# First layer's normalised tokens: turned by VectorE in 32x32 blocks and placed by sixteen transfers, instead of by TensorE

## The reference, cut to what matters

```
x_norm = (x - mean(x)) * rsqrt(var(x) + 1e-6) * ln_scale + ln_bias      # per token, over 128 channels
qkv    = x_norm @ w_qkv + b_qkv                                          # [1024, 128] @ [128, 384]
attn   = softmax(q k^T / 4) over all 1024 tokens, 8 heads of 16
x      = x + (attn v) @ w_out + b_out
```

## Time and profile before

| | us |
|---|---|
| median of three runs | 796.75 |
| the profiled execution | 800.51 |
| its span, first to last instruction | 798.8 |
| TensorE busy (PE) | 758.7 (95%) |
| ScalarE busy (ACT) | 605.2 (76%) |
| VectorE busy (DVE) | 504.5 (63%) |
| GpSimd busy (POOL) | 160.9 (20%) |

### The profile page before, as it was taken

One profiled execution on the slowest core, in us unless ns is written; L12 is line 12 of the kernel. 1 busy time (PEld: TensorE's weight loads), 2 busy tenths in 40 slices (PEclk: granted clock), 3 DMA queues, 4 the chain that ended last, 5 costly groups with the idle time before them and its releaser, 6 DMA issues.

```text
span 798.8 us, 14130 instructions
## 1 busy us (share of the span) xinstructions
PE 758.7 (95%) x4973; PEld 360.5 (45%) x4973; DVE 504.5 (63%) x1512; ACT 605.2 (76%) x686; POOL 160.9 (20%) x198
## 2 busy tenths in 40 slices
PE   8889999999999999999999999999999999898977
PEld 4422333345443545345443545345453455233655
DVE  6514445778467675678657775677726784456864
ACT  4598879787887788787897788878887877777313
POOL 2630504320341020410330212410310201100000
PEclk9999999999999999999999999999999999999999
DMA  2544333432443241622523332422414422400100
GB/s 67 104 78 91 63 62 80 91 63 45 81 95 59 48 80 42 132 51 42 98 61 78 61 61 61 116 51 48 76 32 107 67 48 47 112 6 2 34 1 27
DMA packets 44732, 51.32 MB, mean 64 GB/s; under 512 B 15728, under 2 KB 33776, under 8 KB 44656
## 3 DMA queue, kind: packets, MB, share of 16 engines
q1 hardware_dynamic: 44656, 50.35, 32.6%
HBM read 5.45 MB, written 4.19 MB: 12 GB/s over the span
## 4 chain that ended last, share of the span: by engine, by line
PE 59%; ACT 17%; DVE 6%; issue 6%; ACTq 0%; DVEq 0%
PE O L658 20%; PE S L643 15%; ACT Pr L921 12%; PE BC L672 6%; PE BC L790 3%; PE BC L664 2%; PE BC L713 2%; PE BC L772 2%; PE BC L691 2%; PE A L596 2%; ACT hT L970 1%; ACT tT L936 1%; ACT L921 1%; ACT L970 1%; PE A L672 1%
## 5 line engine op out<-in xcount | busy, mean ns | idle before, releaser
L921 ACT ACTIVATE Pr<-S 128x1024 f32<-128x1024 f32 x512 | 493.0, 1029 | 114.0 <-PE S L643 110.2
L658 PE MATMUL O<-Pr,Va 128*32 128x512 f32 x2048 | 253.5, 602 | 1.1 <-ACT Pr L921 0.9
L643 PE MATMUL S<-Qs,Ks 49*128 49x512 f32 x1024 | 217.3, 469 | 18.0 <-ACT Pr L921 16.0
L643 PEld LDWEIGHTS S<-Qs,Ks 49*128 49x128 f32 x1024 | 87.6, 184 | 178.3 <-ACT Pr L921 138.8
L658 PEld LDWEIGHTS O<-Pr,Va 128*32 128x32 f32 x2048 | 50.3, 109 | 105.4 <-issue 97.5
L1147 DVE STREAM_TRANSPOSE OT<-O 128x512 f32<-128x512 f32 x32 | 22.8, 714 | 54.5 <-PE O L658 54.3
L1252 DVE TENSOR_REDUCE r<-BC 128x1 f32<-128x512 f32 x56 | 36.0, 684 | 21.1 <-PE BC L713 21.1
L485 POOL TENSOR_SCALAR xn<-X,ln 128x128 f32<-128x128 f32 x56 | 44.1, 800 | 4.0 <-DVE ln L1060 4.0
L516 POOL TENSOR_TENSOR squares<-qh 128x1024 bf16<-128x1024 f32 x7 | 13.3, 1895 | 154.3 <-DVE hot L1274 117.8
L524 POOL TENSOR_TENSOR q1l<-q1T,q1h 128x1024 fp32r<-128x1024 f32 x7 | 16.7, 2391 | 133.2 <-DVE q1h L1204 133.2
L538 POOL TENSOR_TENSOR tokx<-tokx_new,tok_bias 128x1024 f32<-128x1024 f32 x8 | 18.9, 2362 | 119.1 <-DVE tokx_new L1066 119.1
(11 more groups left out here) (236 smaller groups left out, 991.3 us busy)
## 6 DMA issues: line engine op xcount, KB each, us to landing
Qs<-qh SPq DMA_DIRECT2D x128, 64.0 KB, 2.3
Ks<-kh SPq DMA_DIRECT2D x128, 64.0 KB, 2.3
Q1s<-q1h SPq DMA_DIRECT2D x56, 128.0 KB, 2.5
X<-in_x_dram SPq DMA_DIRECT2D x8, 512.0 KB, 4.2
Qs<-ql SPq DMA_DIRECT2D x64, 64.0 KB, 2.3
Ks<-kl SPq DMA_DIRECT2D x64, 64.0 KB, 2.3
attnT<-On SPq DMA_DIRECT2D x128, 32.0 KB, 2.0
out_dram<-Y SPq DMA_DIRECT2D x16, 256.0 KB, 2.7
```

The lines of the kernel that those rows point to most:

```text
L643: mm = pe.matmul(S[:, c, a * HALF:(a + 1) * HALF], Ks[head, j, kb * P:(kb + 1) * P], Qs[head, j, c * HALF:(c + 1) * HALF], start=True, sto ...
L658: mm = pe.matmul(O[r:r + 32, :], Va[:, kb, 2 * j + a, :], Pr[:, (STEPS * n + s) % 3, c, a * HALF:(a + 1) * HALF], start=(kb == 0), stop=(k ...
L921: act.activation(Pr[:, g % 3, c, :], S[:, c, :], ACT.Exp, scale=SCALE).then_inc(probs_ready, 1)
```

## The change: what it does

VectorE turns `xn` in 32x32 blocks, two instructions of 128x512 at step 7 of the loop before, into `xb`, which shares the space of `squares`. A block then has its 32 tokens along the free axis, but channel group c of token group g still sits in partitions 32g and columns 32c. Sixteen transfers, one for each g and c, put the blocks where they belong in `xhT`; each moves 32 partitions x 8 tiles x 32 elements, 32 KB in runs of 128 bytes. SyncE issues them in `blocks(n + 1)`, between `load_x(n + 2)` and `attn_out(n, 0)`. At step 11 ScalarE waits for all sixteen and makes `xnT` from `xhT` in one instruction. TensorE's transposes, ScalarE's four drains and the two uses of bank `A` go. This is so for images 1 to 7; image 0's set-up is unchanged.

```diff
--- before.py
+++ after.py
@@ -52,7 +52,7 @@
 
 
 AT_LN0, AT_LN0_FIRST = 11, 22
-AT_XN, AT_XN_SECOND = (11, 15), (8, 10)
+AT_TURN, AT_XNT = 7, 11
 AT_Q, AT_K, AT_V, AT_TOKX = (17, 19), (21, 23), (25, 29), (32, 37)
 AT_BOUND, AT_FLAG = 28, 30
 LIGHT, FULL = 13, 14
@@ -92,11 +92,6 @@
     return n == 0 and s % TILES > 0
 
 
-def xn_steps(n):
-
-    return AT_XN_SECOND if n == 1 else AT_XN
-
-
 WARM = {ENDING.tok: 4, ENDING.t: 4, ENDING.pk: 2, ENDING.sc[0]: 5, ENDING.rt: 8, ENDING.sel: 6, ENDING.pt: 10, ENDING.t2: 10}
 WAKE = 9
 
@@ -110,7 +105,7 @@
     turns = {}
     for g in range(STEPS * (IMAGES + 1)):
         for n in range(1, IMAGES):
-            for use, steps in (("xn", xn_steps(n)), ("q", AT_Q), ("k", AT_K), ("v", AT_V), ("tokx", AT_TOKX),
+            for use, steps in (("q", AT_Q), ("k", AT_K), ("v", AT_V), ("tokx", AT_TOKX),
                                ("bound", (AT_BOUND,)), ("flag", (AT_FLAG,))):
                 for i, s in enumerate(steps):
                     if s == g - STEPS * (n - 1):
@@ -187,6 +182,7 @@
         X, xn = sb("X", [P, TILES, C]), sb("xn", [P, TILES, C])
         xhT, xnT = sb("xhT", [P, T]), sb("xnT", [P, T])
         squares, head_mask_b = sb("squares", [P, 2, T], bf16), sb("head_mask_b", [P, 32], bf16)
+        xb = squares[:, :, :].rearrange("p i t -> p (i t)").bitcast(fp32).rearrange("p (t c) -> p t c", t=TILES)
         warmed = sb("warmed", [1, 1])
         peak, prow, flag = sb("peak", [P, 1]), sb("prow", [1, 256]), sb("flag", [1, 1], i32)
         st0, ln0 = sb("st0", [P, TILES, 6]), [sb(f"ln0_{i}", [P, 8, TILES]) for i in range(2)]
@@ -243,6 +239,7 @@
         half_xn = sem("half_xn")
         first_hi = sem("first_hi")
         x_in = sem("x_in")
+        xn_turned, blocks_in, xnt_ready = sem("xn_turned"), sem("blocks_in"), sem("xnt_ready")
         a_filled, a_drained = sem("a_filled"), sem("a_drained")
         b_filled = [sem("b_filled"), sem("c_filled")]
         b_drained = [sem("b_drained"), sem("c_drained")]
@@ -271,6 +268,7 @@
 
         STACK_DMAS = 2 * (2 * PARTS + 1)
         MAX_TILES = HEADS * TILES
+        BLOCK_DMAS = 16
         QKV_DMAS, FOLD_DMAS, WEIGHT_DMAS = 6, 8, 10 + PARTS
         STACK1_DMAS = PAIRS * PARTS
         ATTN_DMAS = 4
@@ -341,6 +339,19 @@
                         d = 64 * a + HD * part
                         sp.dma_start(Ks[d:d + HD, j, :].bitcast(fp32), k[r:r + HD, :].bitcast(fp32)).then_inc(stack_in[j], 16)
 
+            def blocks(n):
+
+                sp.wait_ge(xn_turned, n)
+                if n > 1:
+                    sp.wait_ge(a_drained, a_after(n - 1, "tokx", 1))
+                else:
+                    sp.wait_ge(first_dve, FIRST_DVE)
+                place = xhT[:, :].rearrange("c (t g q) -> c t g q", t=TILES, g=4)
+                for g in range(4):
+                    for c in range(4):
+                        sp.dma_start(place[32 * c:32 * c + 32, :, g, :], xb[32 * g:32 * g + 32, :, 32 * c:32 * c + 32])\
+                            .then_inc(blocks_in, 16)
+
             def row_maximum(n):
 
                 sp.wait_ge(mneg_ready, n + 1)
@@ -426,6 +437,8 @@
                     sp.sem_inc(mrow_in, 16 * HEADS)
                 if n + 2 < IMAGES:
                     load_x(n + 2)
+                if n + 1 < IMAGES:
+                    blocks(n + 1)
                 attn_out(n, 0)
                 if n > 0:
                     stack1(n - 1)
@@ -479,7 +492,7 @@
                 if n == 1:
                     wait(first_filled, 2)
                 else:
-                    wait(a_filled, a_after(n - 1, "xn", 1))
+                    wait(xn_turned, n - 1)
                 ln = ln0[n % 2]
                 for t in range(TILES):
                     ins = pool.tensor_scalar(xn[:, t, :], X[:, t, :], ln[:, 0, t:t + 1], ln[:, 1, t:t + 1],
@@ -583,15 +596,10 @@
                 mm.then_inc(filled, 1)
 
             def before_tasks(n, s):
-                if s in xn_steps(n):
-                    h = xn_steps(n).index(s)
-                    pe.wait_ge(xn_ready, n + 1)
-                    a_turn(n, "xn", h)
-                    for t in range(4):
-                        mm = pe.transpose(A[:, t * P:(t + 1) * P], xn[:, 4 * h + t, :], ident[:, :])
-                    mm.then_inc(a_filled, 1)
                 if s in AT_Q + AT_K:
                     c, h = (0, AT_Q.index(s)) if s in AT_Q else (C, AT_K.index(s))
+                    if s == AT_Q[0]:
+                        pe.wait_ge(xnt_ready, n)
                     a_turn(n, "k" if c else "q", h)
                     pe.matmul(A[:, :], wqkv_s[:, c:c + C], half(xnT, h), start=True, stop=True).then_inc(a_filled, 1)
                 if s in AT_V:
@@ -921,11 +929,9 @@
                 act.activation(Pr[:, g % 3, c, :], S[:, c, :], ACT.Exp, scale=SCALE).then_inc(probs_ready, 1)
 
             def before_tasks(n, s):
-                if s in xn_steps(n):
-                    h = xn_steps(n).index(s)
-                    act.wait_ge(a_filled, a_after(n, "xn", h))
-                    act.activation(half(xhT, h), A[:, :], ACT.Copy)
-                    act.activation(half(xnT, h), A[:, :], ACT.Identity, bias=LNB, scale=LNS).then_inc(a_drained, 1)
+                if s == AT_XNT:
+                    act.wait_ge(blocks_in, 16 * BLOCK_DMAS * n)
+                    act.activation(xnT[:, :], xhT[:, :], ACT.Identity, bias=LNB, scale=LNS).then_inc(xnt_ready, 1)
 
             def after_tasks(n, s):
                 at = plan(n)
@@ -1089,6 +1095,13 @@
                 return dve.tensor_scalar(flag[:, :], prow[:, 224:225], SAFE_SQUARES, None, ALU.is_gt)
 
             def before_tasks(n, s):
+                if s == AT_TURN:
+
+                    dve.wait_ge(xn_ready, n + 1)
+                    if n > 1:
+                        dve.wait_ge(blocks_in, 16 * BLOCK_DMAS * (n - 1))
+                    dve.transpose(flat4(xb, 0), flat4(xn, 0))
+                    dve.transpose(flat4(xb, 1), flat4(xn, 1)).then_inc(xn_turned, 1)
                 if s in AT_Q + AT_K:
                     h = AT_Q.index(s) if s in AT_Q else AT_K.index(s)
                     if s == AT_Q[0]:
```

## The result

The changed kernel takes 846.35 us at the median (843.60 to 846.63), the kernel before 796.96 beside it: ratio 1.0603, interval 1.0583 to 1.0624, 49 us slower. The prediction was 837.6. The profiled execution took 846.31 us with a span of 844.4, against 798.8 before.

What follows compares the result with a forecast made beforehand. TensorE, busy 95% of the span and alternating with ScalarE, was taken as the bound. Terms 25.8 + 7.9 + 4.4 + 0 + 2.7 = +40.8 us on 800.51 gave 841.3, then 837.6 with the 3.8 median offset; range 822 to 856.

Steps and rivals of the forecast that it cites:

- SyncE's order: Block transfers stand behind X's load in SyncE's queue; loop 0's step 12 waits until 81.3, +25.8 us.
- Pieces: Rival: small pieces or the queue bind, 0.81 us a transfer in every loop, 856 us; chance 17%.
- The clock: TensorE at half rate around the stalls: +1.7 us in loop 0, +1.0 in loop 1, +2.7 together.
- The pass: ScalarE's one 128x1024 instruction from SBUF, replacing the drains: 1.0 us start to start, bounds 0.9 and 1.05.
- Loop 1: Step 12's exps late by 8.4 us, 0.5 back by step 16: +7.9 us.
- Loops 2 to 5: Step 12 late by 2.4 us a loop, 1.3 back: +1.1 each, +4.4 together.
- The cover of `stack1`: SyncE's `stack1`, behind the delayed `attn_out(n, 0)`, waits for q1h anyway: 5.5 us of cover left, cost 0.
- Carrying over the 3.8 us: The median before lay 3.8 us below the profiled execution; the same gap took 841.3 to 837.6.
- VectorE at step 7: Two 128x512 transposes, 1.43 us an image, hidden in 2.19 us of idle time ahead of drains: cost 0.
- The saving: TensorE's two removed groups of transposes: 1.0 us an image, 7 us over 14 groups, the whole possible gain.

Runs made afterwards that it cites:

- e5_warm_full: Changed kernel plus unread full 128-row fp32 matmuls where TensorE idles behind step 12 (10 in loop 1, 1 in loops 2 to 6): 848.64 us.
- e7: Kernel before plus sixteen same-shaped transfers an image at the same place in SyncE's order, whose data nothing computed reads: 804.13 us, ratio 1.0064.
- e1: Changed kernel with image 1's sixteen transfers issued in the set-up, behind the stack of pair 2: 828.39 us, ratio 1.0379.
- e3: Changed kernel with image 1's transfers issued earlier in the set-up, its pass at step 16, and the other images' pass at step 15: 801.77 us.
- e6: Changed kernel with GpSimd, not SyncE, issuing the sixteen transfers, behind its `tokx` addition: 802.41 us, ratio 1.0037.
- e9: Changed kernel with GpSimd issuing the transfers and the pass at step 15 for every image: 790.69 us, ratio 0.9905 to the kernel before.
- e4: Changed kernel plus unread 49-row matmuls where TensorE idles behind step 12 (36 in loop 1, 5 in loops 2 to 6): 848.45 us.
- e8: Changed kernel, but images 1 and 2 turned by TensorE as before; images 3 to 7 by blocks, pass at step 15, SyncE issuing: 793.74 us.

## Why the prediction was right, and where it was small

Sign and cause were right. The time came out 8.7 us above the forecast in the median (846.35 for 837.6) and 5.0 above it in the profiled execution (846.3 for 841.3). It lies inside the stated range of 822 to 856, just above the narrower band, 831 to 845, that had 71%.

**SyncE's order** decided, as forecast. Issues took 0.65 start to start (0.63 predicted), the first behind X 0.74, landing 2.0 for 2.2. In loop 0 the last one started 9.9 us after the first (9.8). Step 12's exps started at 80.56 for 81.3, and the loop lost 27.4 for 27.5. That this agrees to 0.1 is luck: step 12 was 25.2 late for 25.8, and what followed took 2.2 more than before for the 1.7 put down to the clock.

**Pieces** did not bind: landing was no slower than for 16 rows. The sum went by the rows' 0.63 us, and rightly. The 50 ns that the Trainium skill (DMA: Bandwidth & Descriptors, "Anatomy of one DMA — SWDGE (gpsimd) path") gives for the sequencer's part are not what an issue occupies: 0.61 us on SyncE, 0.59 on GpSimd.

**The clock** was a term of its own, +2.7 for loops 0 and 1. In loop 0 TensorE stood idle from 54.9, the granted clock was 0.50 from 58.2 to 89.0, and TensorE was at work again from 81.6.

**The pass** was priced too low: 1.24 us and 1.15 start to start for the predicted 1.0.

**Loop 1** was late by 8.7 (8.4 predicted) and lost 10.4 for 8.9. Behind step 12 it took 56.6 us, and 54.4 in e5_warm_full, where the clock stayed up, for 54.9 before. So 0.5 us came back, as forecast, and the clock cost 2.2 where I put 1.0.

**Loops 2 to 5** are the term of the sum that was mis-sized: +10.3 for +4.4. Step 12 was late by 3.4, 2.7, 3.7 and 2.5 (counted from the loops' starts), 12.4 together for 9.6: in each of these loops one or two of the sixteen issues take 1.0 to 1.6 us (the 11.39 us of loop 3), and the pass is longer. What comes back behind step 12 without half rate is 1.3 to 1.5 a loop, the forecast 1.3. The remaining 3.4 us are the clock in loops 2 and 4 (2.1 and 1.2); I had given the clock these loops only as a bound, and no term of the sum; and that bound, 1.7 a loop, was itself exceeded in loops 1 and 2 (2.2 and 2.1), where the half rate lasted longer than 3.4 us. Where the clock did not fall, +1.1 and +1.3 stood for +1.1.

**The cover of `stack1`** (5.5 us, cost 0) was read in loop 3 and holds there. In loop 1 of the kernel before it is 1.1 us (the stacking lands at 146.70, the scores start at 147.83), as e7 shows with 6.0 us; the forecast took loop 3 for all. In the changed kernel itself the stall at step 11 gave q1 as much delay, so it did not show.

**Carrying over the 3.8 us** between profile and median was wrong: the changed kernel's profiled execution was at its median. The profiled execution of before has a half-rate stretch in loop 7, whose exps take 91.6 us for the changed kernel's 88.7. That is the -2.7 in the table, and would be most of what the median missed beyond the profile; no second execution of before was traced to show it. A window of the kernel before:

```profile
697.00:700.30 3.30, 3.30 (x14) 0.70 (x10) 0.83 (x2) 1.94 (x2) 0.00 (x0) 0.50 0.27 63
```

Loop 7's exps take 88.7 us in the traces of e1 to e3, e6 and e9, which have no such stretch there, and 90.2 to 94.8 in those of e4, e5 and e8, which have one; e7 has 89.8 without one. Over the executions of the kernel before, the mean granted clock goes from 0.985 to 0.998, so how much half rate there is changes from one execution to the next.

**VectorE at step 7** was free, as predicted. ScalarE was busy 7 us less (12 predicted). Its durations fell by 10.9 us (19.6 of drains removed, 8.7 of passes added), but the drains had overlapped each other and the exps, and busy time counts that once.

**The saving** was put at 7 us for all seven images. e9's medians differ by 7.0 (797.73 and 790.69), but its profiled loops 2 to 6 show 5.0 of it and loops 0 and 1 none. That profiled execution was the slowest of e9's six, at a mean granted clock of 0.987; the other five, 3 to 7 us shorter, had 0.991 to 0.998. So the rest may be the clock, which no trace of them shows.

## What to carry to other kernels

When work moves from an engine to transfers, price the queue that issues them: find the time at which it reaches the new entry, in every loop and above all in the first, and what is due behind it. A place that was harmless for transfers nobody needed yet is not harmless for ones that the busiest engine waits for. The same change lost 6% or gained 1%, depending on the queue that issued it and the step at which its result was asked for.

## What the runs showed of the hardware

- A transfer of 32 KB in 256 pieces of 128 bytes costs its issuer 0.61 us on SyncE and 0.59 on GpSimd, and lands in 2.0 us at the median (3.0 from GpSimd); one of 16 rows from SyncE lands in 2.0 too. Of SyncE's issues 22 of 719 in the kernel before and 26 of 831 in the changed one take over 1 us, up to 2.1.
- A half-rate stretch of 3.4 us behind step 12 costs 1.2 to 1.3 us, one of 6.8 costs 2.1 (loops 2 to 4 of four kernels).
- TensorE's clock fell to 0.50 with the engine at 3.40 busy of 3.40 us in matmuls of 49 rows (loop 1 of e4_warm), and held with full ones at that place (e5_warm_full), in one execution each.
- The length of TensorE's idle gap behind step 12's wait does not tell whether half rate follows. In the changed kernel gaps of 1.8 and 2.1 us were followed by it and gaps of 1.1, 0.9 and 0.7 were not; in e4_warm one of 0.9 was, and in e1_first_early one of 2.08 was and one of 2.05 was not.
